# One fused kernel of a recurrent block and a routed feed-forward layer: the order of work around the first expert blocks

## The reference, cut to what matters

```
x  = layernorm(x)                                  # (4, 512, 256)
# recurrent block
h  = rmsnorm(x); a = sigmoid(h @ w_a + bias); g = sigmoid(h @ w_i); v = h @ w_v
s  = sqrt(1 - a*a) * (g * v)
state[t] = a[t] * state[t-1] + s[t]                # along each sequence (written by chunks of 64)
x1 = x + state @ out_proj_w
gate, up = split(rmsnorm(x1) @ w_gate_up)          # 1024 + 1024 columns
out_a = x1 + (silu(gate) * up) @ w_down
# routed layer, over the same normalised x
top 2 of 8 experts by x @ w_router, probabilities by softmax over the two
out_b = sum over the two: prob * (square(relu(x @ w_fc[e])) @ w_proj[e])
return x_original + out_a + out_b
```

## Time and profile before

| | us |
|---|---|
| time before, median of 3 runs (289.14 to 290.12) | 289.37 |
| the profiled execution: its own time | 292.33 |
| the profiled execution: span from first to last instruction | 290.5 |
| TensorE busy in it | 272.2 (94%) |
| VectorE busy | 206.3 (71%) |
| ScalarE busy | 165.9 (57%) |
| GpSimd busy | 114.6 (39%) |

### The profile page before, as it was taken

One profiled execution on the slowest core, in us unless ns is written; L12 is line 12 of the kernel. 1 busy time (PEld: TensorE's weight loads), 2 busy tenths in 40 slices (PEclk: granted clock), 3 DMA queues, 4 the chain that ended last, 5 costly groups with the idle time before them and its releaser, 6 DMA issues.

```text
span 290.5 us, 5331 instructions
## 1 busy us (share of the span) xinstructions
PE 272.2 (94%) x1671; PEld 236.8 (82%) x1671; DVE 206.3 (71%) x420; ACT 165.9 (57%) x361; POOL 114.6 (39%) x136
## 2 busy tenths in 40 slices
PE   5989999999998873999999999999999999999995
PEld 5867778888887763898898788989888899888795
DVE  3899999999676974646559896655657555642994
ACT  3698889967449331346676555447568555532231
POOL 6497016788787510121523332316522242250000
PEclk9999999999999998699999999999999999999999
DMA  6999992248222297231532434423743365019962
GB/s 210 359 387 282 283 329 79 91 137 300 73 92 75 73 132 54 52 63 23 120 65 62 86 69 89 79 50 50 158 95 72 76 97 96 36 56 248 385 235 74
DMA packets 75574, 39.15 MB, mean 135 GB/s; under 512 B 50742, under 2 KB 72252, under 8 KB 75548
## 3 DMA queue, kind: packets, MB, share of 16 engines
q1 hardware_dynamic: 63648, 27.06, 37.2%
q0 software_dynamic: 5520, 11.44, 13.7%
q10 hardware_dynamic: 6380, 0.31, 1.6%
HBM read 22.07 MB, written 16.72 MB: 134 GB/s over the span
## 4 chain that ended last, share of the span: by engine, by line
PE 58%; POOL 17%; DVE 8%; issue 8%; DMA 4%; ACT 2%; ACTq 1%; SPq 0%; DVEq 0%; POOLq 0%
PE ps L407 49%; POOL xs_dram L1530 13%; PE ps L661 3%; DMA sums<-y_dram 2%; PE ps L495 2%; PE ps L411 1%; PE ps L424 1%; DVE hT_lo L1090 1%; DMA xs_dram<-rows_x,slot_u 1%; DMA y_dram<-yb,home_u 1%; PE ps L508 1%; DVE aT_lo L1309 1%; POOL rn L1489 1%; ACT aT_hi L908 1%; ACTq L350 1%
## 5 line engine op out<-in xcount | busy, mean ns | idle before, releaser
L1551 POOL DMA_INDIRECT y_dram<-yb,home_u x39 | 41.2, 1056 | 94.0 <-ACT yb L901 92.2
L1530 POOL DMA_INDIRECT xs_dram<-rows_x,slot_u x32 | 39.7, 1241 | 11.4 <-issue 10.3
L407 PE MATMUL ps<-h2T_lo,Wgu_hi 128*128 128x512 f32 (+1 forms) x132 | 43.0, 389 | 0.0
L407 PE MATMUL ps<-h2T_hi,Wgu_hi 128*128 128x512 f32 (+1 forms) x132 | 41.4, 395 | 0.0
L1309 DVE TENSOR_TENSOR aT_lo<-ps,aT_hi 128x256 fp32r<-128x256 f32 x39 | 16.5, 423 | 34.5 <-ACT aT_hi L908 34.5
L407 PE MATMUL ps<-h2T_hi,Wgu_lo 128*128 128x512 f32 (+1 forms) x132 | 40.8, 390 | 0.0
L407 PE MATMUL ps<-Wd_hi,guT_hi 128*128 128x256 f32 x128 | 36.7, 287 | 2.2 <-DVE guT_lo L1229 2.1
L407 PE MATMUL ps<-Wd_hi,guT_lo 128*128 128x256 f32 x128 | 36.1, 282 | 0.0
L407 PE MATMUL ps<-Wd_lo,guT_hi 128*128 128x256 f32 x128 | 36.1, 282 | 0.0
L1224 DVE TENSOR_TENSOR gu<-gu,ps 128x512 f32<-128x512 f32 x31 | 21.1, 681 | 20.7 <-PE ps L407 16.7
L862 ACT ACTIVATE gu<-ps 128x512 f32<-128x512 f32 x31 | 18.4, 595 | 23.1 <-PE ps L407 21.0
(11 more groups left out here) (175 smaller groups left out, 634.9 us busy)
## 6 DMA issues: line engine op xcount, KB each, us to landing
xs_dram<-blank SPq DMA_DIRECT2D x1, 5160.0 KB, 28.4
xq<-xs_dram SPq DMA_DIRECT2D x156, 32.0 KB
sums<-y_dram SPq DMA_DIRECT2D x8, 512.0 KB, 7.8
Wgu_raw<-in_L_attn_w_gate_up_dram SPq DMA_DIRECT2D x4, 512.0 KB, 9.2
Wfc_raw<-in_L_ffn_w_fc_dram SPq DMA_DIRECT2D x4, 512.0 KB, 10.2
Wpj_raw<-in_L_ffn_w_proj_dram SPq DMA_DIRECT2D x4, 512.0 KB, 6.3
rows_x<-in_L_attn_x_dram SPq DMA_DIRECT2D x3, 512.0 KB, 6.7
rows_x<-in_L_attn_x_dram POOLq DMA_DIRECT2D x3, 512.0 KB, 6.1
```

Of the source, the lines that this page charges most:

```text
L407: return nc.tensor.matmul(dst, lhs, rhs, start=start, stop=stop, skip_group_check=group)
L1530: pool.indirect_dma_start(out=xs_dram, in_=rows_x[:, b, j, :], in_offset=None, out_offset=bass.IndirectOffsetOnAxis(ap=slot_u[:, n:n + 1], ...
L1551: pool.indirect_dma_start(out=y_dram, in_=yb[i % YB][:, :], in_offset=None, out_offset=bass.IndirectOffsetOnAxis(ap=home_u[:, i:i + 1], ax ...
```

## The change

The load of weights and homes is cut in two: slots 0 to 7 (issued by ScalarE behind its half of pair 0) and slots 8 to 39 (issued by SP behind pair 1); homes() is cut alike and moved, part 0 behind the last block of tile 11, part 1 behind block 5. FIRST goes from 10 to 11, tiles 18 and 22 get a third block. cumulate(2, 1) and recur(2, 1) go in front of the blocks. The output projection and the transposes of sequence 1 come one tile earlier on TensorE, with the steps that belong to them on the other engines; the weight halves are spread otherwise over the tiles; root_h2(1) goes in front of the stores of sequence 3's first copies; the first add_x goes from tile 11 to 12.

```diff
-        xq_loaded, of_slot_loaded = [...], sem("of_slot_loaded")
+        xq_loaded, of_slot_loaded = [...], [sem(f"of_slot_loaded{h}") for h in range(2)]
-        FIRST = 10
+        FIRST = 11
         LAST = 24
-        THREE = (12, 14, 16, 19, 24)
+        THREE = (12, 14, 16, 18, 19, 22, 24)
         PROJECT = {11: 2, 17: 3}
         TURN = {13: 2, 20: 3}
-        PROJECT_1, TURN_1 = 4, 6
-        ADD_X = {11: 0, 18: 1, 23: 3}
+        PROJECT_1, TURN_1 = 3, 5
+        ADD_X = {12: 0, 18: 1, 23: 3}
+        OF_SLOT = (slice(0, 8), slice(8, 2 * NP))
+        def load_of_slot(eng, part):
+            eng.dma_start(of_slot[:, OF_SLOT[part], :],
+                          xs_slot[:, OF_SLOT[part], WEIGHT:ROW]).then_inc(of_slot_loaded[part], 16)
 # SP
                 load_pair(sp, n, range(0 if n else P // Q // 2, P // Q))
+                if n == 1:
+                    load_of_slot(sp, 1)
 # ScalarE
             def block_y(i):
-                if i == 0:
-                    act.wait_ge(of_slot_loaded, 16)
+                if i in (0, OF_SLOT[1].start):
+                    act.wait_ge(of_slot_loaded[int(i > 0)], 16)
...
             weights_hi(11)
+            squares(1)
             split_gu(4)
-            squares(1)
             gate(5)
             weights_hi(12)
+            normalise(1)
             split_gu(5)
-            normalise(1)
             gate(6)
+            split_h2(1)
             weights_hi(13)
             split_gu(6)
-            split_h2(1)
+            gate(7)
             weights_hi(14)
-            gate(7)
-            weights_hi(15)
             split_gu(7)
             gate(8)
+            weights_hi(15)
+            split_gu(8)
+            gate(9)
             weights_hi(ALL - 1)
-            split_gu(8)
+            split_gu(9)
             for b in range(B):
                 act.wait_ge(rows_stored[b], 16 * TOP * J)
             load_pair(act, 0, range(P // Q // 2))
-            gate(9)
-            act.dma_start(of_slot[:, :, :], xs_slot[:, :, WEIGHT:ROW]).then_inc(of_slot_loaded, 16)
+            load_of_slot(act, 0)
+            gate(10)
             block_in(0)
 # VectorE: homes(part) does the two steps of homes() on OF_SLOT[part] alone
             split_gu(3)
-            weights_lo(9)
+            add_residual(1, 0)
+            add_residual(1, 1)
             up(4)
             signal(3, 1)
             split_gu(4)
-            add_residual(1, 0)
-            add_residual(1, 1)
+            weights_lo(9)
+            up(5)
             weights_lo(10)
-            up(5)
+            split_gu(5)
             weights_lo(11)
-            split_gu(5)
+            up(6)
+            split_h2(1)
+            split_gu(6)
+            cumulate(2, 0)
+            up(7)
             weights_lo(12)
-            up(6)
-            weights_lo(13)
-            split_gu(6)
-            split_h2(1)
-            weights_lo(14)
-            up(7)
-            cumulate(2, 0)
             split_gu(7)
             recur(2, 0)
             up(8)
+            weights_lo(13)
+            split_gu(8)
+            cumulate(2, 1)
             take_down(0, 0)
             take_down(0, 1)
+            up(9)
+            weights_lo(14)
+            split_gu(9)
+            recur(2, 1)
+            up(10)
             weights_lo(15)
-            split_gu(8)
-            up(9)
-            weights_lo(16)
             block_turn(0)
             block_in(0)
+            weights_lo(16)
...
                         block_in(i + 1)
-                        if i == 0:
-                            homes()
-                            cumulate(2, 1)
-                        if i == 1:
-                            recur(2, 1)
+                        if i == 5:
+                            homes(1)
...
                     block_in(i + 1)
                     if d in TURN:
                         split_h2(TURN[d], range(1, 2))
+                    if d == FIRST:
+                        homes(0)
 # GpSimd
             def scatter(i):
-                if i == 0:
-                    pool.wait_ge(homes_ready, 1)
+                if i in (0, OF_SLOT[1].start):
+                    pool.wait_ge(homes_ready, 1 + int(i > 0))
...
             store_rows(1, 0)
+            root_h2(1)
             store_rows(0, 3)
-            root_h2(1)
             mark_rows(1, 2, 3)
```

More of the change, by code:

```diff
@@ L243, in recurrent_moe_block @@
         sums_loaded, sums_added = [sem(f"sums_loaded{b}") for b in range(B)], sem("sums_added")
-        xq_loaded, of_slot_loaded = [sem(f"xq_loaded{u}") for u in range(XQ)], sem("of_slot_loaded")
+        xq_loaded, of_slot_loaded = [sem(f"xq_loaded{u}") for u in range(XQ)], [sem(f"of_slot_loaded{h}") for h in range(2)]
         homes_ready = sem("homes_ready")
@@ L1274, in add_down, with homes @@
                                     ALU.add).then_inc(out_ready, 1)
-            def homes():
-                dve.wait_ge(of_slot_loaded, 16)
-                at = of_slot[:, :, 1]
-                chain.step(V.scalar_tensor_tensor(out=no_home[:, :], in0=at, scalar=0.0, in1=no_home[:, :],
+            def homes(part):
+                dve.wait_ge(of_slot_loaded[part], 16)
+                mine = OF_SLOT[part]
+                at = of_slot[:, mine, 1]
+                chain.step(V.scalar_tensor_tensor(out=no_home[:, mine], in0=at, scalar=0.0, in1=no_home[:, mine],
                                                   op0=ALU.is_equal, op1=ALU.mult))
-                V.scalar_tensor_tensor(out=home_u[:, :], in0=at, scalar=-1.0, in1=no_home[:, :],
+                V.scalar_tensor_tensor(out=home_u[:, mine], in0=at, scalar=-1.0, in1=no_home[:, mine],
                                        op0=ALU.add, op1=ALU.add).then_inc(homes_ready, 1)
@@ L1592, in _ @@
                         add_x(ADD_X[d])
-                if d in PROJECT or d in TURN:
+                if (d in PROJECT or d in TURN) and block_after(d) >= 3:
                     scatter(block_after(d) - 3)
```

## The result

| | us |
|---|---|
| before, median of 4 runs (289.14 to 290.12) | 289.49 |
| after, median of 4 runs (284.51 to 286.03) | 285.81 |
| ratio | 0.9865, 95% interval 0.9834 to 0.9897 |
| forecast, and its range | 281.8, 280.0 to 285.2 |
| the profiled execution after: own time | 284.51 |

The change made the kernel faster by 3.7 us, where 7.6 were forecast. The direction held, the time lies 0.6 us above the range. Yet the trace's own forecast, the span, held to 0.25 us. In part that is luck: the profiled execution was the fastest of those after, and the spans of the others were 283.8 to 284.3, up to 1.35 above the forecast. The result turns on this difference between one execution and the median.

A forecast was written before the change was run, and what follows sets the result against it. TensorE was taken to set the end, its stalls and clock loss just ahead of tile 12 costing 11.2 us. With 3.6 of new waits, 7.6 came off by stalls (7.55 by spans); off the median 289.37 this gave 281.8, range 280.0 to 285.2.

The forecast's parts named there:

- the trace's own forecast: Whole kernel: the traced span of 290.5 us falls by 7.55 to 282.95.
- the time around the trace: Last step: the traced span's gain of 7.55 us is taken off the median of 289.37, giving 281.8.
- the sum of stalls: TensorE's stalls and clock loss: 11.2 us out, 3.6 of new waits in, 7.6 gained.
- the walk: Engine queues followed from 67.42 us with traced durations; tile 12 starts at 119.3 in place of 131.15.
- the end of the stores: GpSimd's chain of 32 stores: late by 0.3 us at most, last store at 98.6, rows landed at 101.2.
- the stall of 4.94: TensorE before block 0's projection: 5.10 us late, blamed on homes() waiting for of_slot; 2.3 more lost to the clock.
- The new waits: TensorE: 0.56 us at sequence 1's transposes, 1.55 at down(8) for take_down, 0.6 at FC(0).
- two third blocks: Tiles 18 and 22: a third block costs 2.15 us each, 4.3 together.
- A: At down(8), the new 1.55 us gap lowers the clock, costing 2.3: 284.1 us; chance 0.10.
- B: In tiles 6 to 10 the vector engine becomes the bound, 2.7 us more: 284.5; chance 0.13.
- C: Pair 2 lands late behind the homes' loads, delaying tile 12; slower than before 0.05, within 0.3% 0.04.
- D: At the turn of block 2, pair 1 was also late; a stall of 2.5 us remains: 284.3; chance 0.08.

The follow-up runs named there:

- after_again: The changed kernel measured again, unchanged, against the kernel before: 285.32 us (284.86 to 285.83), ratio 0.9804.
- before_addx12: The kernel before with one number changed, the first add_x in tile 12 in place of 11: 286.02 us, ratio 0.9832.
- after_take_first: The changed kernel with take_down of sequence 0 ahead of cumulate(2, 1) on VectorE: 286.7 us, ratio 0.986 to the kernel before.
- before_look5: The kernel before, unchanged, one more traced execution to see its scatter: own time 289.35 us.
- homes_only: The kernel before with only the homes' load and steps cut in two and placed later: 285.22 to 290.63 us, median of all six 289.37.
- after_root_back: The changed kernel with root_h2(1) behind store_rows(0, 3) again: 288.63 us, ratio 0.9878 to the kernel before.
- before_rec_front: The kernel before with only cumulate(2, 1) and recur(2, 1) moved ahead of the blocks: 289.26 us, ratio 0.9941.
- after_addx11: The changed kernel with the first add_x back in tile 11: 287.95 us, ratio 0.9897 to the kernel before.
- after_sp_take: The changed kernel with SP issuing all of pair 0 and both homes parts, and take_down first: 287.65 us, ratio 0.9878 to the kernel before.

## Why the prediction came out as it did

**The failed step: the time around the trace.** "The profiled run took 292.33, the median is 289.37; I take the difference off the median: 281.8". The 7.55 us between the two spans were taken off the median, as if the traced execution's excess of 2.96 stayed in both kernels. It did not. In the kernel before, the executions differ ahead of the mark alone, over 3.3 us; that is the place the change takes apart, and the changed kernel spread over 1 us in after_again. The excess was for the most part in the gain that the trace showed, and had already been counted. One term can be named: the sum of stalls has 1.13 for the transposes of sequence 1, and the four other executions have no wait there. Another 0.6 of the excess lies ahead of that place, at 75.87 against 75.28, and was gone in the executions after, which helped the span by luck: the walk, which starts at 67.42 as in that trace, put the same projection of the changed kernel at 71.66, and it came at 71.16 and, in after_again, at 71.53. The span forecast with the execution's own 1.83 us around it (292.33 - 290.5) gives 282.95 + 1.83 = 284.8; the profiled execution after took 284.51. In own times, trace against trace, the gain is 292.33 - 284.51 = 7.8; between medians it is 3.7, and 5.8 in the second comparison (291.15 to 285.32). The median of three runs, 289.37, was itself on the low side: in the four later comparisons the kernel before had 290.14 to 291.62, so that the traced execution stood only 0.7 to 2.2 above it. How much of that is the other chips and how much the few runs is not shown.

**A smaller one: the end of the stores.** "its chain of 32 stores is late by 0.3 at most: last store 98.6". It was 100.26, and 101.61 in after_again. The walk set the squares' end against the stores of the traced execution, where the store before root_h2 ended near it; the stores ran ahead in the execution after, and GpSimd waited 2.97. In after_again the rows come late enough for ScalarE's wait to hold up gate(10). Its timeline there, with pair 0's four loads, the homes, and gate(10):
```profile
104.25 1.86 ACTq L350 DMA_DIRECT2D xq<-xs_dram  x4
106.14 0.47 ACTq L355 DMA_DIRECT2D of_slot<-xs_dram  x1
106.72 0.60 ACT L870 ACTIVATE gu<-ps 128x512 f32<-128x512 f32 x1 [3.60 <-issue]
```
and on TensorE:
```profile
110.58 0.51 PE L415 MATMUL ps<-Wfc_hi,xgT_hi 128*128 x2 [1.32 <-DVE xgT_lo L1311]
```
VectorE waited 1.3 for that gate, which it did not after. FC(0) is 1.1 later than in the execution after, and so is the mark. It is of the size of the rest between 284.8 and the medians of 285.81 and 285.32; that the other executions differ by the same is not shown by one trace. The walk had "Pair 0 is not what is late there"; of the rows themselves that is right, but the wait for the stores on ScalarE stands ahead of gate(10) too, and in this execution that was late.

**Right time, wrong cause: the stall of 4.94.** That it would go, and the clock with it, held: a clock line of 9s and block 0's projection without a wait. But the cause was credited to the homes' edit, and the removal of add_x(0) was used only to size part 1's load. Moved alone, add_x(0) gives 0.9832; the homes alone give two modes; both give 0.9849. The recurrences alone give 0.9941. These single effects do not add up: each works on the same stall ahead of the mark. The forecast saw queue 0's 512 KB and left it as a remark where it was the main term.

**Where the rest of the steps stand.** The new waits: transposes 0.39 (0.56 forecast, start 83.61 against 84.06, of which 0.5 was there at the projection before it), down(8) 1.60 for take_down (1.55), FC(0) 0.50 at 109.46 (0.6 at 109.75). Tile 12 started at 118.93 (119.3), the seven third-block waits took 3.1 in sum (7 x 0.45), and two third blocks cost 4.35 by the remainders (4.3). The homes' two steps took 0.16 and 0.17 (0.2).

**The shift of the blocks pays nothing by itself.** The mark of the execution after, 114.72, is 12.2 ahead of the traced one before, but only 5.4 ahead of before_addx12's, 120.09. Two blocks have left tile 10, and 4.1 of the 5.4 come back in the remainder, 169.79 against 165.66. That leaves 1.2 us from trace to trace, and 0.9804 against 0.9832 with intervals that overlap: what the rest of the change adds to add_x(0)'s move can't be told from nothing here.

**The rivals.** *A*, the clock at down(8): no, 1.60 of idle left it at 9; yet in after_take_first one gap of 2.21 brought it down, so A was near. *B*, VectorE the bound: down(7) and down(9) were on time; but after_take_first shows that its work ahead of block 0 has no slack left, so B was near. *C*, pair 2 late: between 95 and 135 us VectorE waited for no transfer. *D*, the wait was never the homes: half right. The blocks' rows were as late as the homes in one mode of the kernel before (before_look5) and in homes_only; but with add_x(0) moved, as here, both come in time.

**What stays open.** Which mode the kernel before takes goes with the order of add_x(0) and pair 0, and that with how late the stores end (before_look5, homes_only); why the stores take longer in one execution than in another was not settled. Nor was it tested what the new spread of the weight halves or tile 10 without blocks is worth alone. Only one execution of each variant but these two kernels was profiled, so their marks carry the same doubt as the forecast's.

## What to carry to other kernels

A trace is one execution: before its gain is taken off a median, look in two or three more of the same kernel at which stretch the executions differ in. If that stretch is the one that the change removes, set the trace's own time against the new span, not the median; and give the range room for the new kernel's own scatter, 1.5 us here. When an instruction waits for a small transfer, look at which queue fills the engines in that microsecond: moving a 512 KB transfer that nothing was waiting for gave about as much as the whole rearrangement.

## What the runs showed of the hardware

A plain transfer of GpSimd held the other queues down while it ran: in the kernel before, the homes' queue moved 76 packets in the microsecond in which queue 0 had 98% of the 16 engines, and 1,674 between 108 and 109 us, when queue 0 was through; in before_addx12, 1,916. The indirect stores on GpSimd took 0.96 in some places and up to 2.02 in others, in a pattern that mostly came back from execution to execution. An exception on GpSimd's timeline is the last but one, in the execution after:
```profile
98.99 0.96 POOL L1544 DMA_INDIRECT xs_dram<-rows_x,slot_u  x1 [0.30 <-issue]
```
and in after_again:
```profile
99.36 1.95 POOL L1544 DMA_INDIRECT xs_dram<-rows_x,slot_u  x1 [0.30 <-issue]
```
The granted clock did not follow the length of a gap alone. It fell to half, for 3 us or more each time, at gaps of 4.94 and 4.50 in the kernel before, of 3.75 in before_look5, of 3.46 in after_root_back, of 2.67 in before_rec_front and of 2.21 in after_take_first (the last two with means of 0.994 and 0.992 over the span). It stayed up with 2.94 in homes_only (1.000), 2.69 in after_addx11 (1.000) and 2.60 in after_sp_take (0.999).
